# One decoder layer on one core: four instruction lists per engine instead of one, grouped moments, a 32-bit copy of h, two buffers of probabilities

## The reference

```
x = x + SelfAttention(layernorm(x))          # S: bias by relative position
x = x + CrossAttention(layernorm(x), ctx)    # X: a mask of padded columns
x = x + FFN(layernorm(x))                    # F: 128 -> 2 x 512 -> 128
FFN:  y = quant8(x);  h = silu(y @ Wg) * (y @ Wu);  out = quant8(h) @ Wd
      (weights rounded to -1, 0, 1 times a mean; activations to whole numbers by row)
```

## Time and profile before

| | before |
|---|---|
| three timed runs, us | 458.35, 461.51, 463.34 (median 461.51) |
| profiled execution, span from first to last instruction, us | 457.5 |
| its own time beyond the span | not listed; the fastest run is 0.85 above the span, the median 4.0 |
| busy share of the span | PE 87%, DVE 84%, ACT 79%, POOL 72%, PEld 68% |
| mean granted TensorE clock | 0.959 of full speed |
| bytes moved | 67.27 MB, mean 147 GB/s |

### The profile page before, as it was taken

How to read it: one execution, slowest core, us unless ns; L and a number is a source line. 1 busy time by engine, 2 the same in 40 slices (tenths; PEclk the granted TensorE clock), 3 DMA queues, 4 the chain that set the end, 5 groups by cost and what they waited for, 6 DMA issues and landing times. The chain is left out here.

```text
span 457.5 us, 18022 instructions
## 1 busy us (share of the span) xinstructions
PE 398.0 (87%) x5405; PEld 311.5 (68%) x5436; DVE 385.7 (84%) x1920; ACT 359.9 (79%) x962; POOL 329.2 (72%) x917
## 2 busy tenths in 40 slices
PE   3267879999999999999999999999999999877762
PEld 2245657777777777777877777778877777654430
DVE  4645467999999999999999999999999999888532
ACT  2214758899999999999999999999999998865542
POOL 6834667888888888888888888888888765654120
PEclk9998999999999999999999999999999999998655
DMA  6654577756666766676657675676567662422100
GB/s 190 162 146 100 140 188 184 173 149 172 173 159 160 191 163 168 150 195 172 170 148 196 175 175 153 164 181 170 152 158 189 165 164 80 101 78 77 30 6 13
DMA packets 100181, 67.27 MB, mean 147 GB/s; under 512 B 73269, under 2 KB 90421, under 8 KB 100085
## 3 DMA queue, kind: packets, MB, share of 16 engines
q1 hardware_dynamic: 98209, 64.08, 54.7%
q10 hardware_dynamic: 1876, 2.03, 1.5%
HBM read 46.08 MB, written 19.07 MB: 142 GB/s over the span
## 5 line engine op out<-in xcount | busy, mean ns | idle before, releaser
L895 DVE CUSTOM_DVE_ANT_0 biased<-bank,mask_bias 128x128 bf16<-128x128 f32 x512 | 112.8, 285 | 4.0 <-PE bank L1128 3.9
L900 DVE TENSOR_REDUCE neg_max_S<-bank 128x4 f32<-128x512 f32 x128 | 85.4, 675 | 21.1 <-PE bank L1128 20.4
L599 ACT ACTIVATE probs_S<-bank 128x512 f32<-128x512 f32 x128 | 72.7, 597 | 11.0 <-PE bank L1148 11.0
L599 ACT ACTIVATE probs_X<-bank 128x512 f32<-128x512 f32 x128 | 72.5, 590 | 7.0 <-PE bank L1148 6.4
L1128 PE MATMUL bank<-stack_k_S,stack_q_S 120*128 120x128 bf16 x512 | 50.5, 223 | 11.7 <-DMA stack_k_S<-scratch_S 11.0
L1148 PEld LDWEIGHTS bank<-stack_q_X,stack_k_X 74*128 74x128 bf16 x512 | 41.1, 100 | 16.6 <-issue 2.1
L1128 PEld LDWEIGHTS bank<-stack_k_S,stack_q_S 120*128 120x128 bf16 x512 | 38.6, 102 | 20.1 <-issue 11.9
L1148 PE MATMUL bank<-stack_q_X,stack_k_X 74*128 74x128 bf16 x512 | 51.4, 224 | 0.0
L1145 PE MATMUL bank<-ident_bf,mask_bias 128*128 128x512 bf16 x128 | 50.6, 396 | 0.0
L1128 PE MATMUL bank<-stack_k_X,stack_q_X 72*128 72x128 bf16 x512 | 45.3, 221 | 2.9 <-DMA stack_k_X<-scratch_X 1.7
L1166 PE MATMUL bank<-probs_X,v_aug_X 128*32 128x128 f32 x1024 | 42.4, 285 | 0.0
(11 more groups left out here) (165 smaller groups left out, 1178.6 us busy)
## 6 DMA issues: line engine op xcount, KB each, us to landing
stack_q_S<-scratch_S SPq DMA_DIRECT2D x32, 288.0 KB
stack_k_S<-scratch_S SPq DMA_DIRECT2D x32, 288.0 KB
stack_q_X<-scratch_X SPq DMA_DIRECT2D x32, 288.0 KB
stack_k_X<-scratch_X SPq DMA_DIRECT2D x32, 288.0 KB
scratch_S<-qk_parts_S SPq DMA_DIRECT2D x32, 192.0 KB, 2.7
scratch_X<-qk_parts_X SPq DMA_DIRECT2D x32, 192.0 KB, 2.7
scratch_S<-qk_parts_S SPq DMA_DIRECT2D x32, 64.0 KB, 1.7
ctxT<-ctx SPq DMA_DIRECT2D x8, 256.0 KB, 4.7
```

The lines of the kernel that those rows point to most:

```text
L599: act.activation(probs[a][:, c, :], bank_b[c % 2][:, :], ACT.Exp).then_inc(sems["exp_" + a], 1)
L895: last = dve.tensor_tensor_reduce(biased[:, c, hh, :], quarter(bank_a[c % 2], hh), mask_bias[:, b % 2, :], -1.0, -2.0 * BIG, ALU.add, ALU.min,
L900: dve.tensor_reduce(neg_max[a][:, first_head(c):first_head(c) + 2 * HC - 1:2], bank_a[c % 2][:, :].rearrange("i (h j) -> i h j", h=HC), AX ...
```

## The change

Each engine gets **four lists**: `fill` for steps -1 to 2 (self-attention alone), `ramp` for the next 6, `step` for 28, `drain` for the rest. The orders and lags are all new. The cross-attention's counter x now starts three steps behind the self-attention's. `due` keeps track of what each entry has done, so that an entry whose lag changes between two lists neither skips nor repeats a batch.

- *Moments in groups.* The 32 batches of x are treated in 9 groups (1, 3, then 4 each): `ln_group` on DVE, three small operations per group on POOL. All moments for S are due by the third ramp step. The six later loads of x go out one per step from the first step on (`load_x`), instead of one every four steps.
- *h as 32-bit words.* `hT_out` copies the transposed float16 pairs as 256 float32 words instead of converting 512; the 1536 stays in, and `down` takes it off by a fifth matmul with the column sums of the weights, made once on DVE. w_down becomes float16.
- *Two buffers of probabilities.* `exp` of batch b waits for `attend` of b - 2, not of b - 1.
- The additions of constants in `yT_out` and `quantise_h` use an immediate number instead of a column. `take` waits for all readers of a PSUM bank's last contents instead of a written-out list.
- At the start, the split of the relative positions comes before the moments of batch 1, and ACT's three loads of the relative rows (`rel_rows`) come behind batch 1's `part2` instead of batch 0's.

The core of the diff; the lists shown are those the prediction speaks of:

```
-STEPS = [(t, t) for t in range(-1, B + 10)]
+LEAD, RAMP, TAIL, LAGS = 3, 6, 5, 12
+MOMENTS = (0, 1, 4, 8, 12, 16, 20, 24, 28, 32)
...
+        def run(begun, fill, ramp, step, drain):
+            for s in range(-1, LEAD):
+                fill(Step(s, None, begun))
+            for x in range(RAMP):
+                ramp(Step(x + LEAD, x, begun))
+            for x in range(RAMP, B + TAIL - LEAD):
+                step(Step(x + LEAD, x, begun))
+            for x in range(B + TAIL - LEAD, B + TAIL + LAGS):
+                drain(Step(x + LEAD, x, begun))
...
+            def ln_group(st, lag):                                     # DVE
+                for g in st.due("S", lag, "ln_group", n=len(MOMENTS) - 1):
...
+                        dve.bn_stats(stats_s[:, b - lo, :], x_all[:, b, :]).then_inc(sems["stats_S"], 1)
+                    for b in range(lo, hi):
+                        dve.wait_ge(sems["stats_S"], b + 1)
+                        dve.bn_aggr(mv_s[:, b, :], stats_s[:, b - lo, :]).then_inc(sems["mv_S"], 1)
...
+                    if b >= 2:                                          # ACT, exp
+                        act.wait_ge(sems["av_" + a], done(b - 2, CH, c + 1))
+                    act.activation(probs[a][:, b % 2, c, :], bank_b[c % 2][:, :], ACT.Exp)
...
-                act.activation(hT[:].rearrange("p c s -> p (c s)"), bank_t[:, 0:256].bitcast(F16), ACT.Identity,
-                               bias=minus_round16[:, 0:1]).then_inc(sems["hT"], 1)
+                    copy(hT[:].rearrange("p c s -> p (c s)").bitcast(F32), bank_t[:, 0:256]).then_inc(sems["hT"], 1)
...
+                    last = pe.matmul(bank_t[:, 256:384], minus_offset[:], w_down_sum[:], start=False, stop=True)
...
+            def fill(st):                                               # PE
+                xn_transposed("S", st, -1)
+                scores_b("S", st, 2, 3)
+                scores_a("S", st, 1, 2)
+                scores_a("S", st, 1, 3)
+                attend("S", st, 2, 0)
+                attend("S", st, 2, 1)
+                project_qkv("S", st, -1)
+                attend("S", st, 2, 2)
...
+                max_transposed("S", st, 1)
+                attend("S", st, 2, 3)
+                o_transposed("S", st, 2)
+                scores_b("S", st, 1, 0)
+                scores_a("S", st, 0, 0)
...
+                on_transposed("S", st, 2)
+                scores_b("S", st, 1, 1)
+                scores_a("S", st, 0, 1)
+                scores_b("S", st, 1, 2)
+                project_out("S", st, 2)
...
             def step(st):                                               # PE
+                scores_b("S", st, 3, 1)
+                project_out("S", st, 4)
+                xn_transposed("X", st, 2)
+                o_transposed("X", st, 5)
+                scores_b("S", st, 3, 2)
+                max_transposed("X", st, 4)
+                project_qkv("X", st, 2)
+                on_transposed("X", st, 5)
+                scores_a("S", st, 2, 1)
+                scores_b("S", st, 3, 3)
...
+                gate_up(st, 5)
+                scores_a("S", st, 1, 0)
+                attend("X", st, 4, 0)
+                attend("X", st, 4, 1)
+                attend("X", st, 4, 2)
+                attend("X", st, 4, 3)
+                scores_b("S", st, 2, 0)
...
+            def step(st):                                               # DVE, its middle list
+                ln_group(st, -2)
+                ternary_weights(st, 1)
+                row_max("S", st, 1, 0)
+                gate(st, 5)
+                gated(st, 5)
...
+                row_max("S", st, 1, 3)
+                row_max("X", st, 2, 0)
...
+            def step(st):                                               # SP, its middle list
+                max_in("X", st, 3)
+                stack_in("S", st, 0)
+                parts_again("X", st, 1)
...
+                stack_in("X", st, 1)
```

More of the change, by code:

```diff
@@ L58, with __init__, due, at @@
 class Step:
[L61 to L70, removed]
+    def __init__(self, s, x, begun):
+        self.newest = {"S": s, "X": x, "F": x}
+        self.begun = begun
+    def due(self, stage, lag, *key, n=B):
+        if self.newest[stage] is None:
+            return range(0)
+        first = self.begun.get((stage, key), 0)
+        end = max(first, min(self.newest[stage] - lag + 1, n))
+        self.begun[stage, key] = end
+        return range(first, end)
+    def at(self, s):
+        return self.newest["S"] == s
 def layer(nc, x, ctx, mask, w_self, w_cross, w_ffn, w_down, cols, w_out_s, w_out_x, bo_rows,
@@ new lines, in store @@
+            def store(st, lag):
+                for b in st.due("F", lag, "store"):
+                    if b < B - GROUP and b % GROUP != GROUP - 1:
+                        continue
+                    n = GROUP if b < B - GROUP else 1
+                    batches = slice(b + 1 - n, b + 1)
+                    sp.wait_ge(sems["res_F"], done(b))
+                    sp.dma_start(out[batches].rearrange("b s d -> s b d"), x_all[:, batches, :])\
+                        .then_inc(sems["out_stored"], 16)
@@ L365, in _, with drain @@
+            def drain(st):
+                store(st, 7)
+                parts_out("X", st, -48)
+                stack_in("X", st, -16)
+                max_in("X", st, 0)
+                parts_again("X", st, -24)
+            run(begun, fill, ramp, step, drain)
             sp.wait_ge(sems["out_stored"], 16 * (B // GROUP - 1 + GROUP))
@@ L370, in _ @@
             n = 0
+            begun = {}
             def const(instruction):
@@ L1071, in _ @@
+            rel_split()
+            run(begun, fill, ramp, step, drain)
         @block.tensor
         def _(pe):
+            begun = {}
             pe.wait_ge(sems["qkv_loaded"], 16 * 2)
@@ new lines, in o_transposed @@
+            def o_transposed(a, st, lag):
+                for b in st.due(a, lag, "o_transposed"):
+                    if a == "S" and b == 0:
+                        pe.wait_ge(sems["ffn_const"], MEAN_W)
+                    pe.wait_ge(sems["o_raw_" + a], done(b))
+                    take("t", ("o_norm_" + a, done(b)))
+                    for half in range(2):
+                        last = pe.transpose(quarter(bank_t, half), o_raw[a][:, half, :], ident[:])
+                    last.then_inc(sems["o_ps_" + a], 1)
```

1712 lines of the change are left out of this document (911 added, 801 removed).

## The result

The changed kernel took 467.52 us (median of 4 runs, 466.81 to 468.41), the kernel before 460.31 beside it (458.35 to 463.34): a ratio of 1.0165, 95% interval [1.0127, 1.0204]. It is slower by 1.7%. The forecast of 454.5 us, faster, was wrong, and 467.52 lies outside its range of 443 to 465.

The account below looks back on a forecast made before the run. The prediction took DVE to bound the middle, stack latency the filling and a chain between gates the end: 457.5 - 9.1 - 6.3 + 8.5 = 450.6 us of span, times 1.0088 gives 454.5 us in the runs; range 443 to 465.

Parts of the forecast that it names:

- Filling, -9.1: Filling, up to the last maxima of S batch 6: ends at 83.5 us instead of 92.57, 9.1 us gained.
- Middle, -6.3: Middle, 25 batches: S moments leave DVE's list, so a step takes 11.55 us instead of 11.80, 6.3 us gained.
- h as words, 0: Middle: ACT's copy of h gets 0.30 us shorter per batch, but beside DVE's work, so nothing is gained there.
- Second buffer of probabilities, 0: The second buffer removes a wait of which DVE sees nothing, so it gains 0.
- End, +8.5: End, behind the last maxima of S: seven gates remain instead of six, 78.4 us against 69.9, 8.5 us lost.
- four intervals of 10.6: End: four of the intervals between the seven gates take 10.6 us each, the shortest before at full clock.
- Rival 2: Middle: PE bounds it, so the 0.25 us per step are not gained; 460.9 us in the runs, chance 0.08.
- The rule weighed there: Middle: PE's weight loading (79%), not its busy share (97.8%), shows its limit; sum 450.6 us, by busy share 456.9.
- Rival 3: Middle: self-attention's stacks arrive late, PE waits; at 1 us per step 480 us in the runs, chance 0.15.
- Rival 1: Filling: keeps its pace, still limited by the stacks; 463.7 us in the runs, chance 0.17.
- or if a wait of DVE appears in the middle: Middle: a sign that the forecast is wrong, besides the filling gaining under 3 us.

Follow-up runs that it names:

- e8: Changed kernel with the X remainder moved behind the feed-forward normalisation in POOL's middle list: 477.44 us.
- e4: Kernel before with the S moments left out from batch 8 on, 0.32 us less on DVE per step: ratio 0.9989 to the kernel before.
- e10: Changed kernel with ACT's copy of X's first parts moved ahead of the last S exponential in the middle list: ratio 1.0049 to the kernel before.
- e2: Changed kernel with one unused bn_stats and bn_aggr put back on DVE per middle step, 0.32 us more: ratio 1.0230 to the kernel before.
- e6: Changed kernel with half of three S row maxima left out, 0.79 us less on DVE per step: 467.56 us.
- e5: Changed kernel with half the columns of four exponentials left out, 0.85 us less on ACT per step: 460.76 us.
- e9: Kernel before with only h transposed moved as 32-bit words, 0.30 us less on ACT per step: ratio 1.0037 to the kernel before.
- e12: Changed kernel with h transposed copied as 512 numbers of 16 bits again: ratio 1.0150 to the kernel before.
- e3: Changed kernel with ten unread matmuls in each of the three steps x = 31, 32, 33: ratio 1.0100 to the kernel before.
- e11: Changed kernel with the edits of e10 and e3 together: 460.35 us, ratio 1.0017 to the kernel before.
- e16: e11 with unread matmuls also in the first three steps of the drain list: 457.94 us, ratio 0.9947 to the kernel before.
- e1: Changed kernel with a zero mask and without four mask matmuls, 0.85 us less on PE per step: ratio 1.0177 to the kernel before.
- e7: Changed kernel with the three savings of e1, e5 and e6 on PE, ACT and DVE together: 466.53 us.
- e13: Kernel before with a zero mask and without four mask matmuls, 0.85 us less on PE per step: 458.11 us.
- e14: Changed kernel with two chunks of the second X scores moved behind the X projection in the three steps without S work: ratio 1.0176 to the kernel before.

## Why the prediction was wrong, step by step

- **Filling, -9.1: right in size on the mean, 5.5 us in the profiled pair.** The moments of S do run there, the last bn_stats at 67.5 us, and PE waits only once more for a stack of S, 0.3 us. The first scores of S batches 0, 3 and 6:

```profile
24.48 1.03 PE L1289 MATMUL bank<-stack_k_S,stack_q_S 120*128 120x128 bf16 x8 [5.74 <-DMA stack_k_S<-scratch_rel]
...
49.10 0.39 PE L1289 MATMUL bank<-stack_k_S,stack_q_S 120*128 120x128 bf16 x4
...
81.50 0.39 PE L1289 MATMUL bank<-stack_k_S,stack_q_S 120*128 120x128 bf16 x4
```

  The start is 1.0 us earlier than the forecast's 25.5, the first three batches took 24.6 us against 25.2, the next three 32.4 against 28.7 (at a granted clock of 0.84 and 0.85 in the last two), and the last maxima came 5.6 us behind the first scores instead of 4.1. In e8, at a clock of 1.00, S b6 ended at 82.8, against 83.5. That the means differ by 9.4 is in part luck: both fillings end later on the mean than the figures that the forecast took, by 2.7 and 2.3 us.
- **Middle, -6.3: failed.** It is the largest miss, 7.1 of the 16.0 us between the forecast's span and the measured one (filling 3.6, end 5.3), and by itself takes the gain away: 450.6 + 7.1 = 457.7. The prediction said "In the middle DVE is the bound" and "A better order of another engine gives nothing here; only work taken off DVE does". Both halves are false. The moments alone, taken off DVE in the kernel before, give nothing (e4), and a better order on ACT gives 0.26 us per step in the changed kernel (e10). It took DVE's 97.0% for a bound. In its place the runs show, in the changed kernel, a step that follows the ring over ACT, POOL and PE (e10), with a path through DVE close behind it (0.32 us more on DVE cost 0.28, e2). What held the 11.78 before stays open, but it was not DVE's sum. The Trainium skill, Perfetto Trace Analysis, "Identifying the Most-Contended Engine", says to take the engine of highest occupancy as the most contended and to optimise it first, where TensorE is judged by its weight loading. The runs disagree for this kernel: DVE has the highest share by that rule (94% of the middle, 97% before), and 0.79 us less on it (e6), or 0.32 less before (e4), gave nothing; the 0.2 that e5 gave on ACT is the saving of one instruction on the ring.
- **h as words, 0: right**, by e9 and e12, though not for the reason given, cover by DVE, which falls with e4 and e6. The copy itself fell from 687 ns to 392, as costed.

```profile
L682 ACT ACTIVATE hT<-bank 128x256 f32<-128x256 f32 x19 | 7.5, 392 | 0.0
```

- **Second buffer of probabilities, 0:** not tried by itself.
- **End, +8.5: right in its mechanism, too small.** Seven gates remain, as counted. The term "four intervals of 10.6" failed: they took 11.33, 13.69, 14.12 and 12.61, 9.4 us more; the last two took 9.10 and 9.59 where it had 11.0, 3.3 us less; the first gate and what follows the last come to 13.3 instead of 14.0. I had put the low clock in the last two steps, and the full clock in the four before them. In this profile some 5.8 us of the 9.4 are the clock in x = 32 and 33 (e3), about 1.2 more in x = 34 (12.17 in e11, 10.98 in e16); at full clock the four would still have taken 11.33 + 11.21 + 10.79 + 10.98 = 44.3 instead of 42.4, an estimate from the profiles of the changed kernel, e3 and e16. Where the clock fell less, in e2, the whole end took 78.5 us, the forecast's 78.4, but by errors that cancel: the four took 46.1 and the last two 19.1.
- **Rival 2** (the middle unchanged) had the right number for the middle and the wrong cause: PE did not bound it, as e1, e7 and e13 show. The rule weighed there, that weight loading and not the busy share tells PE's limit, stands: at 177.73 of 224 us, 79%, PE was not the limit in e1, so the trace agrees. But from "PE is not at its limit" I concluded that DVE is. **Rival 3** did not come: PE's first scores wait for no stack of S in the middle. **Rival 1** did not come either.
- The sign "or if a wait of DVE appears in the middle" came. What DVE lost in work, 6.3 us, came back as waits in small pieces: in 118 to 342 us its listed waits grew from 0.4 us in 2 pieces to 7.0 in 21, the largest entry 3.4 us in 14 pieces for POOL's normalised row of F. The distance of the gates shows the failure more plainly.

Not settled: what held the step of the kernel before (above), whether it is chance that both kernels come to nearly the same step, why the clock falls in one execution and not in another, what makes single steps of the changed kernel a few tenths to 1.5 us longer (mean of the distances 11.85, median 11.76; 11.66 and 11.50 in e10), and how much one step less of depth between S and F would give. That would shift every lag of the lists and was not tried.

## What to carry to other kernels

When several engines are all busy for 77 to 98% under fixed orders, don't price a change by the fullest engine: follow one period back through what each instruction really waited for, and price only what lies on the ring. Look at an engine with idle time that waits in every step for the same instruction and for little else; it may be part of the bound. And count what a deeper pipeline leaves behind: its extra steps at the end run thin, at whatever clock a thin PE is granted.

## What the runs showed of the hardware that was not expected

- Unread work can save time: with ten matmuls of 512 columns in each of three steps the clock stayed at 1.00 in four profiles of four, where it had fallen to 0.50 for 19.5 us in the changed kernel. By the ratios this took 0.65% off (e3), and three more steps with them another 0.7% (e16 against e11).
- The same lists can be granted different clocks from one execution to the next. The filling of nine kernels that differ only behind it ended up to 7 us apart (82.8 us at a clock of 1.00, 90.1 at 0.91, both in 24 to 80 us), and the thin steps at the end took 39.1 us in the changed kernel and 33.5 in e2 without any unread work, while the median step of the kernels with the same middle list (the changed kernel, e3, e14) agrees to 0.01 us. One profile is enough for a step, and not for a filling or an end.
